# Node maxima of a graph attention layer: destination terms split and keyed during the gathers, maxima in two halves, copies shared with ScalarE

## The chip, the cores and the metric

One NeuronCore of a Trainium2 chip runs the whole program in one launch. The metric is the device time of that core in microseconds (us). TensorE is called PE, VectorE DVE, ScalarE ACT, GpSimd POOL and SyncE SP. The engines run their own instruction streams and meet at semaphores; each stage of the kernel is a block that ends with a barrier over all engines.

## The reference, cut to what matters

Two graph layers on 6250 nodes (128 features) and 106,250 edges sorted by destination. The change touches the first layer's attention, for 4 relations and 8 heads:

```python
es = einsum('nhd,hd->nh', x, a_s); ed = einsum('nhd,hd->nh', x, a_d)      # x = node_inp @ W[r]
logit = leaky_relu(es[src] + ed[dst], 0.2)
logit = where(mask[:, None], logit, -1e30)        # mask: edges of relation r
mx = maximum(segment_max(logit, dst, num_segments=N), -1e30)
p = exp(logit - mx[dst]) * mask[:, None]
alpha = p / segment_sum(p, dst)[dst]
out = segment_sum(alpha[..., None] * x[src], dst)
```

Leaky ReLU grows with its argument and `ed[dst]` is the same for all edges of a destination, so `mx` is `leaky(max(es[src]) + ed)`: the maximum over edges needs only the source terms. The kernel uses this.

## The kernel before, in words

`lists` builds the schedule, `node_inputs` makes the source and destination terms of every node, and `relation_maxima` runs a segmented maximum of the source terms along the sorted edges and stores the running maxima in HBM (`T.run`, 32 floats an edge: 4 relations x 8 heads). Then comes `node_maxima`, the stage that is changed, and after its barrier `relation_attention`, the stage that uses its results; `node_update` and the second layer follow.

`node_maxima` holds nodes as 50 tiles of 128 (a tile is a column of 128 partitions).

- POOL issues 50 indirect DMAs (L857), one a tile: each partition fetches the running maximum at its node's last edge, 32 floats, into `run`. All increment one semaphore.
- DVE first makes `none` (L863: 0 for a node that has edges, -1e30 otherwise), copies the destination terms `K.ed` into slot 0 of `both` (L866) and clears the accumulator `acc` of the next stage (L867, 27,200 floats a partition). Then it waits for all 50 gathers.
- In 5 chunks of 10 tiles it adds `none` (L872), tests which relations are present (L874), adds `ed` (L876) and applies the leaky ReLU into slot 1 of `both` (L877). Each instruction of a chain waits for the one before it (`L.link`).
- `both`, 3200 floats a partition, is then written as a sum of TERMS = 3 bf16 numbers. For each term i: cast to `term` (L885), subtract it from `both` (L887, not for the last), and 16 copies (L890) that bring `term` from node order (partition = node within the tile) to key order in `K.edm` (partition = relation x 32 + node within a window of 32). The copy for (q, r) takes partitions 32q to 32q+31 of `term` and writes partitions 32r to 32r+31 of `K.edm`: 50 tiles x 16 bf16. The next term's cast waits for all 16.
- SP loads two small index tables (L850, L851). ACT and PE have nothing to do in this stage.

`relation_attention` starts with a load of key rows by ACT (L1020) and of edge rows by SP (L930); `K.outside`, a float array of `relation_maxima`, is dead by then and its space holds the edge rows.

Every term of the DVE chain is on the way to the barrier once the gathers have landed. The order of instructions on each engine is the order in which the source writes them.

Of the kernel before, what the change touches and what calls it, by code (L numbers as in the profile page):

```python
# [4 lines left out]
F32, I32, BF16 = mybir.dt.float32, mybir.dt.int32, mybir.dt.bfloat16  # L5
ALU = mybir.AluOpType
ACT = mybir.ActivationFunctionType
# [3 lines left out]
P = 128  # L11
N_NODES, N_EDGES = 6250, 106250
C = 128
R, H, D = 4, 8, 16
# [5 lines left out]
TILES = 50  # L20
# [4 lines left out]
KWIN = 32  # L25
# [11 lines left out]
TERMS = 3  # L37
# [8 lines left out]
BIG = 1e30  # L46
SLOPE0, SLOPE1 = 0.2, 0.01
# [3 lines left out]
def flat(ap):  # L51
    return ap.rearrange("p a b -> p (a b)")
# [776 lines left out]
def node_maxima(nc, K, T, acc):  # L829

    with Phase(nc, "top") as ph:
        CH = 10
        S2 = 2 * H
        run = ph.sb("run", [P, TILES, R * H])
        none = ph.sb("none", [P, TILES])
        both = ph.sb("both", [P, TILES, R, 2, H])
        term = ph.sb("term", [P, TILES, R, 2, H], BF16)
        s_run, s_keyed = (ph.sem(n) for n in ("run", "keyed"))
        s_w, w_all = ph.loads(K, 2)
        block = ph.block()  # L840
        KQ = P // KWIN
        quads = [(q, r) for q in range(KQ) for r in range(R)]

        def to_keys(q, r, i):
            out = K.edm[r * KWIN:(r + 1) * KWIN, :, i * S2:(i + 1) * S2].rearrange("k (t q) c -> k t q c", q=KQ)[:, :, q, :]
            return out, term[q * KWIN:(q + 1) * KWIN, :, r, :, :].rearrange("p t s h -> p t (s h)")

        @block.sync
        def _(sp):
            sp.dma_start(K.reg_kw[:, :], T.ksched_w.rearrange("(a s) -> a s", a=1)).then_inc(s_w, 16)  # L850
            sp.dma_start(K.reg_ke[:, :], T.ksched_e.rearrange("(a s) -> a s", a=1)).then_inc(s_w, 16)  # L851
            sp.wait_ge(s_w, w_all)

        @block.gpsimd
        def _(pool):
            for t in range(TILES):
                pool.indirect_dma_start(run[:, t, :], None, T.run,  # L857
                                        bass.IndirectOffsetOnAxis(ap=K.last[:, t:t + 1], axis=0)).then_inc(s_run, 16)

        @block.vector  # L860
        def _(dve):
            L = K.setup.on(dve)
            L.link(dve.tensor_scalar(none[:, :], K.has[:, :], 1.0, BIG, ALU.subtract, ALU.mult))  # L863
            ed4 = K.ed[:, :, :].rearrange("p t (r h) -> p t r h", r=R)
            run4 = run[:, :, :].rearrange("p t (r h) -> p t r h", r=R)
            L.mark(dve.tensor_copy(both[:, :, :, 0, :], ed4))  # L866
            L.mark(dve.memset(acc[:, :, :], 0.0))  # L867
            dve.wait_ge(s_run, 16 * TILES)
            for c in range(0, TILES, CH):
                k = slice(c, c + CH)  # L870
                wr = "p t r h -> p (t r) h"
                L.link(dve.tensor_tensor(run4[:, k, :, :], run4[:, k, :, :],  # L872
                                         none[:, k].unsqueeze(2).unsqueeze(3).to_broadcast([P, CH, R, H]), ALU.add))
                L.mark(dve.tensor_scalar(K.valid[:, k, :], run4[:, k, :, 0], -0.9 * BIG, None, ALU.is_gt))  # L874
                L.wait()
                L.link(dve.tensor_tensor(run4[:, k, :, :], run4[:, k, :, :], ed4[:, k, :, :], ALU.add))  # L876
                L.mark(dve.scalar_tensor_tensor(both[:, k, :, 1, :], run4[:, k, :, :], SLOPE0, run4[:, k, :, :], ALU.mult, ALU.max))  # L877
            L.wait()
            all4 = "p t r s h -> p (t r s h)"
            rest = both[:, :, :, :, :].rearrange(all4)  # L880
            for i in range(TERMS):
                part = term[:, :, :, :, :].rearrange(all4)
                if i:
                    dve.wait_ge(s_keyed, i * len(quads))
                L.link(dve.tensor_copy(part, rest))  # L885
                if i < TERMS - 1:
                    L.mark(dve.tensor_tensor(rest, rest, part, ALU.subtract))  # L887
                for q, r in quads:
                    out, src = to_keys(q, r, i)
                    dve.tensor_copy(out, src).then_inc(s_keyed, 1)  # L890
                L.wait()
            dve.wait_ge(s_keyed, TERMS * len(quads))


def relation_attention(nc, K, T, acc):

    with Phase(nc, "att") as ph:
        U, RG = U4, 4
        GROUPS = KSTEPS // U
        S2 = 2 * H  # L900
        xe = flat(K.outside[:, :, :])[:, 0:RG * U * XW].rearrange("p (b u c) -> p b u c", b=RG, u=U)
        keyrow = ph.sb("keyrow", [P, RG, U * P], BF16)
        away = ph.sb("away", [P, U * P])
        keyT = ph.sb("keyT", [P, RG, U * P], BF16)
        dv = ph.sb("dv", [P, U, S2])
        keys = ph.sb("keys", [P, RG, U])
# [5 lines left out]
        px = ph.sb("px", [P, 2, U, XR])  # L912
        dst_ps = [ph.ps(f"dst_ps{b}", [P, U, TERMS * S2]) for b in range(2)]
        sum_ps = [[ph.ps(f"sum_ps{b}{q}", [P, 2, XR]) for q in range(U // 2)] for b in range(2)]
# [33 lines left out]
        def _(dve):  # L948
# [3 lines left out]
            def select(j, b, step):  # L952
# [13 lines left out]
                else:  # L966
                    dve.wait_ge(s_sc, j * 3 + 3)
                    if past(j, RG):
                        dve.wait_ge(s_p, j - RG + 1)
                    dve.tensor_tensor(arg[:, b, :, :], leaky[:, :, :], dv[:, :, H:S2], ALU.subtract).then_inc(s_arg, 1)  # L970

# [88 lines left out]
def node_update(nc, K, T, acc):  # L1060

    with Phase(nc, "upd") as ph:
        CH = 4
        bias = ph.sb("bias", [P, C])
        RT = 4
        zero = ph.sb("zero", [P, 4 * HID])
        rden = ph.sb("rden", [P, RT, CH, H])
        tmp = ph.sb("tmp", [P, RT, CH, C])
        s_b, s_c, s_n, s_g, s_gd, s_z, s_zd = (ph.sem(n) for n in ("b", "c", "n", "g", "gd", "z", "zd"))
# [766 lines left out]
def build(nc, T):  # L1836
# [6 lines left out]
    with Phase(nc, "k") as ph:  # L1843
# [13 lines left out]
        with Phase(nc, "l0") as l0:  # L1857
            K.key = l0.sb("key", [P, P * KKC])
            K.last, K.has = l0.sb("last", [P, TILES], I32), l0.sb("has", [P, TILES])
            K.ed, K.valid = l0.sb("ed", [P, TILES, R * H]), l0.sb("valid", [P, TILES, R])  # L1860
            K.index, K.outside = l0.sb("index", [P, NB], I32), l0.sb("outside", [P, NB, R])
            lists(nc, K, T)
            node_inputs(nc, K, T)
            relation_maxima(nc, K, T)
            acc = l0.sb("acc", [P, KSLOTS, XR])
            with Phase(nc, "l0a") as l0a:
                K.reg_kw, K.reg_ke = l0a.sb("reg_kw", [1, P * KKC], I32), l0a.sb("reg_ke", [1, P * KKC], I32)
                K.edm = l0a.sb("edm", [P, KSLOTS, TERMS * 2 * H], BF16)
                node_maxima(nc, K, T, acc)
                relation_attention(nc, K, T, acc)  # L1870
            node_update(nc, K, T, acc)
# [59 lines left out]
```

## Time and profile before

| | |
|---|---|
| median of 3 runs | 5624.1 us (5619.86 to 5625.64) |
| profiled execution, time | 5625.34 us |
| its span | 5623.5 us |
| busy share of the span | DVE 69%, POOL 69%, PE 59%, PEld 41%, ACT 25% |
| the stage `node_maxima` in the trace | about 1441 to 1547 us |

How to read it: the rows below are from one profiled execution. In the timeline view the columns are start (us), duration (us), engine, line, operation, output<-input, count; in brackets stands how long the engine sat idle before it and what released it. In the view of one tile the three durations are minimum, median and maximum in ns. "issue" is time in which the engine waited for nothing that the profile shows.

### The profile page before, as it was taken

The page shows a single profiled execution, that of the slowest core. Times are in us where ns is not written, and L with a number is a line of the kernel's source. Part 1 is how long each engine was busy: PE and PEld are TensorE (multiplying, and loading weights), DVE is VectorE, ACT ScalarE, POOL GpSimd, SP SyncE. Part 2 cuts the span into 40 slices and gives each one's busy share as a digit, 9 for nine tenths or more (in the row PEclk, how much of TensorE's full clock was granted, in tenths as well). Part 3 has the DMA queues.
Part 4 walks back from the last instruction along what each step waited for, and adds up shares of the span by engine and source line. Part 5 has one row for each costly group of instructions (what it writes and reads, how often), then busy time and mean ns, then how long its engine had stood idle before and what let it go on. Part 6 is the DMA issues. An engine that isn't in the chain of part 4 may idle for free. (4 is left out here: it accounts for less than half of the span.)

```text
span 5623.5 us, 106320 instructions
## 1 busy us (share of the span) xinstructions
PE 3324.9 (59%) x16923; PEld 2283.8 (41%) x16924; DVE 3907.1 (69%) x11806; ACT 1426.7 (25%) x2966; POOL 3884.4 (69%) x3803
## 2 busy tenths in 40 slices
PE   0062222222066677155777777777777777777768
PEld 0031111111056566143444444444444455544447
DVE  4635555555578888896777777777777777777765
ACT  0130000000066666334222222222222222222222
POOL 3127777777499999520677777777777777777760
PEclk9885555555577777577888888888889998888889
DMA  2266666666166666323787777877888878778864
GB/s 57 58 186 192 196 195 194 195 193 195 46 154 154 155 153 154 114 49 117 183 176 174 175 172 173 176 173 173 175 175 176 176 174 174 173 172 174 174 141 143
DMA packets 725286, 893.97 MB, mean 159 GB/s; under 512 B 123241, under 2 KB 555465, under 8 KB 724710
## 3 DMA queue, kind: packets, MB, share of 16 engines
q0 software_dynamic: 217200, 396.10, 34.5%
q1 hardware_dynamic: 450742, 392.89, 24.4%
q10 hardware_dynamic: 56976, 101.87, 5.9%
q14 instruction: 357, 2.92, 0.2%
q8 instruction: 11, 0.18, 0.0%
HBM read 652.36 MB, written 238.06 MB: 158 GB/s over the span
## 5 line engine op out<-in xcount | busy, mean ns | idle before, releaser
L1529 POOL DMA_INDIRECT sums<-msg_bsum,k_sidx x831 | 1320.8, 1589 | 378.0 <-issue 242.1
L731 POOL DMA_INDIRECT max_xe<-rows,l_index x832 | 798.5, 960 | 427.0 <-issue 253.3
L1664 PEld LDWEIGHTS msg_both_ps<-msg_onehot,msg_hid 128*128 128x128 f32 x3712 | 555.6, 207 | 1312.5 <-DVE msg_bsum L1573 852.5
L1629 ACT ACTIVATE msg_low_ps<-msg_xs 128x512 f32<-128x512 f32 x928 | 558.1, 601 | 2084.5 <-DVE msg_xs L1598 2049.5
L1543 POOL DMA_INDIRECT msg_ga<-ab,k_bsrc x832 | 827.4, 994 | 369.2 <-issue 201.9
L1677 PE MATMUL msg_pre_ps<-msg_rw,msg_lt 128*128 128x512 f32 x1856 | 1019.0, 632 | 9.5 <-DMA msg_rw<-ab 9.5
L1664 PE MATMUL msg_both_ps<-msg_onehot,msg_hid 128*128 128x64 f32 x3712 | 619.0, 293 | 618.8 <-DVE msg_bsum L1573 602.5
L942 POOL TENSOR_SCALAR att_keyhot<-k_ramp,att_keys 128x128 f32<-128x128 f32 x1028 | 701.6, 701 | 55.6 <-ACT att_keys L1014 54.8
L1608 DVE TENSOR_TENSOR msg_hid<-msg_xs,msg_low_ps 128x512 f32<-128x512 f32 x928 | 636.7, 686 | 97.6 <-ACT msg_low_ps L1629 70.5
L1666 PE MATMUL msg_both_ps<-msg_hid,msg_same 128*128 128x256 f32 x1856 | 653.6, 436 | 0.0
L1597 DVE TENSOR_TENSOR msg_xs<-msg_pre_ps,msg_ga 128x256 f32<-128x256 f32 x928 | 390.1, 420 | 370.0 <-issue 252.9
L1054 PE MATMUL att_sum_ps<-att_px,att_keyhot 128*128 128x136 f32 x2056 | 434.7, 370 | 143.8 <-DVE att_px L976 136.7
L1573 DVE SCALAR_TENSOR_TENSOR msg_bsum<-msg_bsum,l_cont,msg_both_ps 128x256 f32 x928 | 441.2, 475 | 4.8 <-issue 0.2
L1054 PEld LDWEIGHTS att_sum_ps<-att_px,att_keyhot 128*128 128x128 f32 x2056 | 366.3, 255 | 177.4 <-DVE l_acc L986 121.5
L814 PE MATMUL max_mT_ps<-k_ident,max_m 128*32 128x128 f32 x832 | 194.0, 413 | 386.6 <-DVE max_m L748 386.6
L1598 DVE TENSOR_TENSOR msg_xs<-msg_pre_ps,msg_ga 128x256 f32<-128x256 f32 x928 | 385.6, 416 | 3.7
L1677 PEld LDWEIGHTS msg_pre_ps<-msg_rw,msg_lt 128*128 128x128 f32 x1856 | 359.8, 204 | 59.1 <-issue 10.5
L986 DVE TENSOR_TENSOR l_acc<-l_acc,att_sum_ps 128x136 f32 x1028 | 299.5, 291 | 121.1 <-issue 78.8
L748 DVE TENSOR_TENSOR max_m<-max_xe,l_outside 128x256 f32<-128x256 f32 x104 | 44.3, 426 | 441.8 <-DMA max_xe<-rows,l_index 441.8
L823 PE MATMUL max_runT_ps<-k_ident,max_run 32*128 32x32 f32 x832 | 106.9, 288 | 379.7 <-DVE max_run L761 379.7
L1666 PEld LDWEIGHTS msg_both_ps<-msg_hid,msg_same 128*128 128x128 f32 x1856 | 306.9, 208 | 0.0
L802 ACT ACTIVATE max_runT<-max_runT_ps 128x256 f32<-128x256 f32 x104 | 39.8, 383 | 1025.8 <-PE max_runT_ps L823 1025.8
(292 smaller groups left out, 5373.3 us busy)
## 6 DMA issues: line engine op xcount, KB each, us to landing
msg_rw<-ab SPq DMA_DIRECT2D x928, 128.0 KB
l_outside<-xe SPq DMA_DIRECT2D x1028, 72.0 KB, 2.7
xe<-max_xe SPq DMA_DIRECT2D x104, 576.0 KB, 3.0
max_src<-srcs ACTq DMA_DIRECT2D x104, 512.0 KB, 3.9
att_keyrow<-key ACTq DMA_DIRECT2D x257, 128.0 KB, 3.5
msg_lt<-in_efT SPq DMA_DIRECT2D x928, 32.0 KB
rows<-node_rows SPq DMA_DIRECT2D x50, 288.0 KB, 2.4
max_begin<-begin ACTq DMA_DIRECT2D x104, 128.0 KB
```

The source lines that it names most:

```text
L731: pool.indirect_dma_start(xe[:, b, u, :], None, T.rows, bass.IndirectOffsetOnAxis(ap=K.index[:, k:k + 1], axis=0)).then_inc(s_xe[b], 16)
L942: pool.tensor_scalar(keyhot[:, b, u, :], K.ramp[:, 1:P + 1], keys[:, b, u:u + 1], None, ALU.is_equal).then_inc(s_kh, 1)
L1054: pe.matmul(sum_ps[b % 2][u // 2][:, u % 2, :], keyhot[:, b, u, :], px[:, b % 2, u, :], start=True, stop=True).then_inc(s_sum, 1)
L1529: pool.indirect_dma_start(T.sums[k % 2], bass.IndirectOffsetOnAxis(ap=K.sidx[:, k:k + 1], axis=0), bsum[:, (k + 1) % SB, :], None, compute ...
L1543: pool.indirect_dma_start(ga[:, (k + 1) % RB, :], None, T.ab, bass.IndirectOffsetOnAxis(ap=K.bsrc[:, k:k + 1], axis=0)).then_inc(s_ga[k % ...
L1573: dve.scalar_tensor_tensor(row, row, K.cont[:, ds(n, 1)], bwd_ps[u % 2][:, :], ALU.mult, ALU.add).then_inc(s_bs, 1)
L1597: dve.tensor_tensor(xs[:, u % 2, 0:HID], pre_ps[u % 2][:, 0:HID], row[:, HID:2 * HID], ALU.add)
L1608: dve.tensor_tensor(hid[:, b % 2, u, :], xs[:, u % 2, :], low_ps[u % 2][:, :], ALU.max).then_inc(s_hid, 1)
L1629: act.activation(low_ps[u % 2][:, :], xs[:, u % 2, :], ACT.Copy, scale=SLOPE1).then_inc(s_low, 1)
L1664: pe.matmul(fwd_ps[u % 2][:, q * WIN:(q + 1) * WIN], hid[:, b % 2, u, HID + q * P:HID + (q + 1) * P], onehot[:, b, u, :], start=True, stop ...
L1666: pe.matmul(bwd_ps[u % 2][:, :], same[:, b % 2, u, :], hid[:, b % 2, u, 0:HID], start=True, stop=True).then_inc(s_edge, 1)
L1677: pe.matmul(pre_ps[u % 2][:, :], lt[:, b, u, :], rw[:, b % 2, u, :], start=True, stop=True).then_inc(s_pre, 1)
```

## The change

The destination terms and the maxima are no longer joined in `both`. There are three parts: part 0 is the destination terms of all 50 tiles, parts 1 and 2 are the maxima of tiles 0 to 24 and 25 to 49. Each part is split into its three bf16 terms in one go (`split`), with `term` large enough that nothing is overwritten, and then copied to key order; slot s of a term now has its own copy (8 bf16 a tile where it was 16), so that there are 3 parts x 3 terms x 16 = 144 copies where there were 48. DVE does q = 0, 1 and ACT q = 2, 3, 24 copies a part each. Part 0 is done before the memset and before the wait for gathers; its float remainder lies in the space of `K.outside`. The gathers of the two halves have a semaphore each. The chain of none, presence, ed and leaky is done on 25 tiles at a time, in place in `run`.

```diff
+        rest = flat(K.outside[:, :, :])[:, 0:TILES * RH].rearrange("p (t c) -> p t c", t=TILES)
-        both = ph.sb("both", [P, TILES, R, 2, H])
-        term = ph.sb("term", [P, TILES, R, 2, H], BF16)
+        term = ph.sb("term", [P, 2, TERMS, TILES, RH], BF16)
...
+        parts = [(0, slice(0, TILES)), (1, slice(0, HALF)), (1, slice(HALF, TILES))]
+        def to_keys(s, i, k, q, r):
+            c = (2 * i + s) * H
+            out = K.edm[r * KWIN:(r + 1) * KWIN, :, c:c + H].rearrange("k (t q) c -> k t q c", q=KQ)[:, k, q, :]
+            return out, term[q * KWIN:(q + 1) * KWIN, s, i, k, r * H:(r + 1) * H]
...
-                                        bass.IndirectOffsetOnAxis(ap=K.last[:, t:t + 1], axis=0)).then_inc(s_run, 16)
+                                        bass.IndirectOffsetOnAxis(ap=K.last[:, t:t + 1], axis=0)).then_inc(s_run[t // HALF], 16)
+        @block.scalar
+        def _(act):
+            for g, (s, k) in enumerate(parts):
+                act.wait_ge(s_term, g + 1)
+                for i in range(TERMS):
+                    for q in range(KQ // 2, KQ):
+                        for r in range(R):
+                            out, src = to_keys(s, i, k, q, r)
+                            act.activation(out, src, ACT.Copy).then_inc(s_keyed, 1)
...
+            def split(g, values):
+                s, k = parts[g]
+                for i in range(TERMS):
+                    part = term[:, s, i, k, :]
+                    ins = dve.tensor_copy(part, values[:, k, :])
+                    if i < TERMS - 1:
+                        L.link(ins)
+                        L.link(dve.tensor_tensor(values[:, k, :], values[:, k, :], part, ALU.subtract))
+                    else:
+                        ins.then_inc(s_term, 1)
+                dve.wait_ge(s_term, g + 1)
+                for i in range(TERMS):
+                    for q in range(KQ // 2):
+                        for r in range(R):
+                            out, src = to_keys(s, i, k, q, r)
+                            dve.tensor_copy(out, src).then_inc(s_keyed, 1)
+
+            L.mark(dve.tensor_scalar(none[:, :], K.has[:, :], 1.0, BIG, ALU.subtract, ALU.mult))
+            L.link(dve.tensor_copy(rest[:, :, :], K.ed[:, :, :]))
+            split(0, rest)
             L.mark(dve.memset(acc[:, :, :], 0.0))
-            dve.wait_ge(s_run, 16 * TILES)
-            for c in range(0, TILES, CH):
...
+            for g in range(1, len(parts)):
+                s, k = parts[g]
+                n = k.stop - k.start
+                dve.wait_ge(s_run[g - 1], 16 * n)
+                L.link(dve.tensor_tensor(run[:, k, :], run[:, k, :], none[:, k].unsqueeze(2).to_broadcast([P, n, RH]), ALU.add))
+                L.mark(dve.tensor_scalar(K.valid[:, k, :], run[:, k, 0:RH:H], -0.9 * BIG, None, ALU.is_gt))
                 L.wait()
...
+                L.link(dve.tensor_tensor(run[:, k, :], run[:, k, :], K.ed[:, k, :], ALU.add))
+                L.link(dve.scalar_tensor_tensor(run[:, k, :], run[:, k, :], SLOPE0, run[:, k, :], ALU.mult, ALU.max))
+                split(g, run)
             L.wait()
...
+            dve.wait_ge(s_keyed, KEYED)
```

## Rows read from the trace of the kernel before

**Rows 1.** The page: busy us of each engine, share of the span, instructions.

```profile
PE 3324.9 (59%) x16923; PEld 2283.8 (41%) x16924; DVE 3907.1 (69%) x11806; ACT 1426.7 (25%) x2966; POOL 3884.4 (69%) x3803
```

**Rows 2.** Busy us by stretch: from:to, length, each engine, PE clock, DMA share, GB/s.

```profile
1438.00:1507.00 69.00, 0.54 (x6) 0.40 (x4) 26.10 (x19) 0.38 (x1) 47.65 (x50) 0.50 0.08 14
1507.00:1515.50 8.50, 0.00 (x0) 0.00 (x0) 7.97 (x20) 0.00 (x0) 0.00 (x0) 0.50 0.00 0
1515.50:1547.00 31.50, 0.00 (x0) 0.00 (x0) 29.55 (x53) 0.00 (x0) 0.00 (x0) 0.50 0.00 0
```

**Rows 3.** Timeline, the start of the stage.

```profile
1441.20 0.19 DVE L863 TENSOR_SCALAR top_none<-l_has 128x50 f32<-128x50 f32 x1 [0.94 <-PEq L181]
1441.43 0.99 DVE L866 COPY top_both<-l_ed 128x1600 f32<-128x1600 f32 x1
1441.82 1.42 POOL L857 DMA_INDIRECT top_run<-run,l_last  x1 [12.81 <-PEq L181]
1448.04 22.73 DVE L867 MEMSET l_acc<- 128x27200 f32 x1 [5.61 <-issue]
```

**Rows 4.** Timeline, from the last gather's landing to the next stage.

```profile
1506.97 0.49 DVE L872 TENSOR_TENSOR top_run<-top_run,top_none 128x320 f32<-128x320 f32 x1 [36.21 <-DMA top_run<-run,l_last]
1507.49 0.20 DVE L874 TENSOR_SCALAR l_valid<-top_run 128x40 f32<-128x40 f32 x1
...
1515.52 1.83 DVE L885 CAST top_term<-top_both 128x3200 bf16<-128x3200 f32 x1
1517.38 3.49 DVE L887 TENSOR_TENSOR top_both<-top_both,top_term 128x3200 f32<-128x3200 f32 x1
1520.79 6.23 DVE L890 COPY l0a_edm<-top_term 32x800 bf16<-32x800 bf16 x16
...
1540.57 6.23 DVE L890 COPY l0a_edm<-top_term 32x800 bf16<-32x800 bf16 x16
1547.37 1.30 ACTq L1020 DMA_DIRECT2D att_keyrow<-key  x3
```

**Rows 5.** The view of tile run: the gathers and their time to landing.

```profile
L857 POOL DMA_INDIRECT top_run<-run,l_last x50: 940/944/1424, 1441.8 to 1503.5; - x50
...
DMA to landing us min/median/max: 2.2/2.4/3.5
```

**Rows 6.** The view of tile term: the copies to key order.

```profile
L890 DVE COPY l0a_edm<-top_term x48: 349/360/367, 1520.8 to 1546.4; 32x800 bf16<-32x800 bf16 x48
```

**Rows 7.** Timeline, early in the program: other gathers beside long DVE instructions.

```profile
24.06 3.79 DVE L467 TENSOR_TENSOR list_begin<-list_rec 104x1024 f32<-104x1024 int32 x1
26.18 2.74 POOL L399 DMA_INDIRECT list_dst<-in_dst,list_block_i  x1 [0.18 <-issue]
27.88 0.69 DVE L468 TENSOR_SCALAR list_begin<-list_begin 104x1024 f32<-104x1024 f32 x1
28.49 1.96 DVE L469 SCALAR_TENSOR_TENSOR list_index<-list_rec 104x1024 f32<-104x1024 int32 x1
29.21 2.09 POOL L399 DMA_INDIRECT list_dst<-in_dst,list_block_i  x1 [0.30 <-issue]
```

**Rows 8.** Timeline, in relation_maxima: a gather beside short DVE instructions.

```profile
704.42 0.35 DVE L769 SCALAR_TENSOR_TENSOR max_junk<-max_src,max_srcf,k_upto 128x128 bf16<-128x128 f32 x1
704.53 1.06 POOL L731 DMA_INDIRECT max_xe<-rows,l_index  x1 [0.30 <-issue]
```

**Rows 9.** Groups by line and shape on ACT: busy us, mean ns, idle before.

```profile
L1117 ACT ACTIVATE l_acc<-upd_tmp 128x512 f32 x44 | 27.7, 630 | 55.5 <-POOL upd_tmp L1108 55.5
L627 ACT ACTIVATE node_squares<-node_x 128x3200 f32<-128x3200 f32 x2 | 5.7, 2870 | 30.8 <-DVE node_x L595 30.8
L438 ACT ACTIVATE k_loc<-list_tp_ps 128x512 f32<-128x512 f32 x2 | 2.0, 1131 | 0.0
```

**Rows 10.** Timeline of ACT, two instructions in a row with no wait.

```profile
1992.38 0.72 ACT L1030 ACTIVATE att_keyT<-att_away,k_ones 128x512 bf16<-128x512 f32 x1
1993.01 0.19 ACT L1014 ACTIVATE att_keys<-l_key 128x4 f32 x1
```

More of the change, by code:

```diff
@@ L831, in node_maxima @@
     with Phase(nc, "top") as ph:
-        CH = 10
-        S2 = 2 * H
-        run = ph.sb("run", [P, TILES, R * H])
+        HALF = TILES // 2
+        KQ = P // KWIN
+        RH = R * H
+        run = ph.sb("run", [P, TILES, RH])
+        rest = flat(K.outside[:, :, :])[:, 0:TILES * RH].rearrange("p (t c) -> p t c", t=TILES)
         none = ph.sb("none", [P, TILES])
-        both = ph.sb("both", [P, TILES, R, 2, H])
-        term = ph.sb("term", [P, TILES, R, 2, H], BF16)
-        s_run, s_keyed = (ph.sem(n) for n in ("run", "keyed"))
+        term = ph.sb("term", [P, 2, TERMS, TILES, RH], BF16)
+        s_run = [ph.sem(f"run{q}") for q in range(2)]
+        s_term, s_keyed = (ph.sem(n) for n in ("term", "keyed"))
         s_w, w_all = ph.loads(K, 2)
         block = ph.block()
[L841 to L846, printed above, removed]
+        parts = [(0, slice(0, TILES)), (1, slice(0, HALF)), (1, slice(HALF, TILES))]
+        KEYED = len(parts) * TERMS * KQ * R
+        def to_keys(s, i, k, q, r):
+            c = (2 * i + s) * H
+            out = K.edm[r * KWIN:(r + 1) * KWIN, :, c:c + H].rearrange("k (t q) c -> k t q c", q=KQ)[:, k, q, :]
+            return out, term[q * KWIN:(q + 1) * KWIN, s, i, k, r * H:(r + 1) * H]
         @block.sync
@@ L862, in _ @@
             L = K.setup.on(dve)
[L863 to L866, printed above, removed]
-            L.mark(dve.memset(acc[:, :, :], 0.0))
-            dve.wait_ge(s_run, 16 * TILES)
-            for c in range(0, TILES, CH):
[L870 to L874, printed above, removed]
+            def split(g, values):
[14 more added lines that the diff above has]
+                            dve.tensor_copy(out, src).then_inc(s_keyed, 1)
@@ L875, in _ @@
                 L.wait()
-                L.link(dve.tensor_tensor(run4[:, k, :, :], run4[:, k, :, :], ed4[:, k, :, :], ALU.add))
-                L.mark(dve.scalar_tensor_tensor(both[:, k, :, 1, :], run4[:, k, :, :], SLOPE0, run4[:, k, :, :], ALU.mult, ALU.max))
+                L.link(dve.tensor_tensor(run[:, k, :], run[:, k, :], K.ed[:, k, :], ALU.add))
+                L.link(dve.scalar_tensor_tensor(run[:, k, :], run[:, k, :], SLOPE0, run[:, k, :], ALU.mult, ALU.max))
+                split(g, run)
@@ L878, in _ @@
             L.wait()
[L879 to L891, printed above, removed]
@@ L892, in _ @@
-            dve.wait_ge(s_keyed, TERMS * len(quads))
+            dve.wait_ge(s_keyed, KEYED)
 def relation_attention(nc, K, T, acc):
```

## The prediction

> **What bounds the kernel now.** I read the page first: no engine is busy for more than 69% of the span [rows 1], so the kernel is a row of stages with different limits, and only the changed stage's own limit counts. The busy time by stretch shows it: from 1438 to 1507 us POOL is busy 47.65 of 69 us with 50 gathers, and from 1507 to 1547 DVE alone works (7.97 of 8.5, 29.55 of 31.5) and every other engine and the DMA stand at 0 [rows 2]. The timeline puts edges on it: the gathers start at 1441.82, the last is issued at 1503.5 and landed at 1506.97, when DVE had been idle for 36.21 us [rows 3 to 5]; the last copy ends about 1546.8 and the next stage begins at 1547.37 [rows 4]. So the stage is gathers (65.5 us), then a serial DVE tail (39.8 us); both are on the path, and the cover of one engine by another in it is nil.
>
> One row needs care. The memset is shown as 22.73 us after 5.61 us in which DVE waited for nothing [rows 3]. Their sum, 28.34 us, is 27,200 elements at 0.96 a ns, so I take it that the memset runs from 1442.42 to 1470.77 and its start is recorded late. I use 28.3 us.
>
> **Durations.** From the copy of 1600 floats, 0.99, and the cast of 3200, 1.83 [rows 3, 4], a one-input DVE instruction on floats costs 0.162 + 0.52 us per 1000; from 320 at 0.49 and 3200 at 3.49 a two-input one costs 0.157 + 1.042 per 1000 [rows 4]. The key copy of 800 bf16 takes 0.360 [rows 6]; with the same fixed part it is 0.25 per 1000, so 400 take 0.26 and 200 take 0.21. Sixteen of them span 6.23 us, a pitch of 0.391, thus 0.031 beyond the duration. Chained instructions start 0.03 after the end before them (1506.97 + 0.49 to 1507.49) [rows 4].
>
> **The tail that stays behind the last gather (part 2).** Chain on 800 floats: five two-input instructions (none, ed, leaky, two subtractions) at 0.99, three casts at 0.58, presence 0.23; with 0.03 after each of the nine, 4.95 + 1.74 + 0.23 + 0.27 = 7.2 us. Then DVE has 24 copies of 200 elements at 0.24, 5.7 us, and ACT 24 beside it. The trace has no ACT copy of this shape. From 512 floats at 630 ns and 3200 at 2870 ACT costs 0.203 + 0.833 per 1000 [rows 9], 0.37 for 200. ACT instructions without a wait start 0.09 before the end of the one in front (0.63 after 1992.38 where the duration is 0.72) [rows 10]; where partitions change, DVE loses such an overlap [rows 6], and ACT may too. The pitch is therefore 0.28 to 0.40, and I take 0.34, the middle, since neither row is nearer: 8.2 us. If ACT pays for short pieces as it does for a scattered output (512 elements in 1131 ns, 1.81 per 1000 [rows 9]), it is 0.56, 13.5 us. The pieces here are 8 neighbours long, nearer to the plain rows, so this end is for the range. ACT ends last: tail 7.2 + 8.2 = 15.4 us where it was 39.8. That removes **24.4 us** (bounds: DVE's own 12.9, 26.9 saved; scattered ACT, 19.1 saved).
>
> **What moves ahead of that.** Part 0 on DVE: the copy of 1.0 us was there already; new are three casts at 0.99 and two subtractions at 1.83, with gaps 6.8 us, and 24 copies at 0.29, 7.0 us. The memset moves behind it, to about 1456.3 to 1484.6. Part 1 is 7.2 + 5.7 = 12.9 us, to 1497.5; its 25 gathers would land by 1476, so the memset, not the gathers, decides when it starts. All of this must fit before the last landing, 1506.97, and does with 9.5 us to spare. ACT's copies (24 of 400 elements, at 0.45 to 0.57, and 24 of 200) fit in the same cover, and ACT is idle here. If that cover were gone, every us beyond 9.5 would be one on the path. SP's two loads are untouched; queued behind DVE's new instructions are only the memset and its own chain. The barrier is now released by ACT's last copy through DVE's wait, about 0.1 us. The second half's semaphore changes nothing for the last landing.
>
> **What it costs POOL.** The price of the cover is that DVE now works beside the gathers, where before only one copy and the memset did. The rows show what that does. The first gather, beside the copy, took 1.42 against a median of 0.944: it ended 0.82 after that copy [rows 3, 5]. An earlier one took 2.74 beside a two-input and then a one-input instruction and ended 0.35 after the second; the next took 2.09 and ended 0.85 after a two-input one [rows 7]. Beside 0.35-us instructions a gather loses 0.1 (1.06) [rows 8]. Beside the memset (no input) the gathers keep 0.94 [rows 5]. A reading that fits: 0.09 us in, a gather needs a read that any DVE instruction with two inputs or with a fast copy holds up until its end; 0.5 us later it needs writes, some 0.35 us, which only the fast one-input kind holds up.
>
> Stepping the gathers with this through part 0's chain: they start at 1441.82, 1444.1, 1447.0 and 1449.9, where the fourth started at 1446.04 before: +3.8 us. Through part 1's chain the same steps give 5 gathers in 8.3 us instead of 6.25: +2.0. Beside the back-to-back copies (7.0 + 5.7 us, with 0.03 between them) the trace has nothing; from below 0.1 a gather [rows 8], some 1 us in all; from above no progress at all, 12.7 us. I take 0.35 for each of some 8 gathers (half a copy's wait for the read, one for the writes), 2.8 us, near the lower end because rows 8 is the only case of short instructions. Sum **+8.6 us**; bounds 1.0 and 18.5.
>
> The Trainium skill has a stricter rule (SBUF — State Buffer, Who interferes with whom): a Vector copy or cast in a two-port mode takes the pair of ports shared with GpSimd for the whole instruction, and the other "fully blocks", the descriptors of a gather included. The 1.42 and 2.74 above agree with that. The page does not say how a run of short ones shares; taken as lock-out for all DVE work in the two parts it is the third rival.
>
> **Sum.** Profiled execution 5625.34 (span 5623.5) - 24.4 + 8.6 = 5609.5. The median of the runs shown lies 1.2 below it: 5608.3. I forecast **5609 us**, 16 us faster (0.28%). Nothing behind the barrier changes but its start.
>
> **Rivals.**
> 1. The gathers are not noticeably held up (+1): 5601. For: gathers at 0.94 beside the memset and at 1.06 beside short ones. Against: the 1.42, 2.74 and 2.09. Chance 0.17.
> 2. The copies starve the gathers nearly wholly (+14 to 18), or ACT pays for short pieces on top: gain 3 to 10, 5614 to 5621, say 5618. For: 0.03 us gaps leave POOL little. Against: rows 8. Chance 0.27.
> 3. The other side: every DVE instruction of parts 0 and 1 locks POOL out for its whole length, 6.8 + 7.0 + 7.2 + 5.7 = 26.7 us. It decides once the last landing slips by more than 24.4 us: 5625.3 + 2.3 = 5627.6, and with ACT at 0.56 5633. Against: a gather beside a two-input instruction finished within 0.85 of its end, so it isn't set back, and its last part runs beside such instructions. Chance 0.05.
> 4. The change doesn't do what it says: ACT's copies wait for something, or part 1 starts late (the memset ends after the gathers), so that parts 1 and 2 run one after another: 12.9 us more in the tail, 5622. The 9.5 us of slack speaks against it. Chance 0.03.
>
> The forecast itself has 0.48.
>
> **Chances.** A difference below 0.2%, 11.2 us, is what a measurement of this kernel can tell from none. Faster by more: the forecast nearly whole and rival 1, 0.63. Within 0.2%: rival 2, 3, 4 and the forecast's upper edge, 0.34. Slower by more than 0.2%: 0.03, since even the lock-out with a dear ACT stays below 5635. The range that holds the time 8 times in 10 is 5600 to 5621.
>
> **What would show it.** The last gather landing near 1515.6 instead of 1506.97, with gathers of 1.2 to 2.5 us beside part 0 and part 1 and 0.94 beside the memset; DVE copies of 0.26 and 0.21 us; ACT copies of 0.37 at a pitch of 0.28 to 0.40; from the last landing to the first load of the next stage 15.5 us. Wrong would be: gathers that need over 3 us beside copies (rival 2), a landing at 1508 (rival 1), an idle ACT between copies, or a DVE that is still busy with part 1 when the last gather lands.

## The result, and where the time went

The changed kernel takes 5586.8 us (median of 5; 5579.8 to 5603.2) against 5625.5 for the kernel before (5 runs, 5619.9 to 5630.9): ratio 0.9937, 95% interval 0.9919 to 0.9955. That is 38.7 us faster where 16 were forecast, and below the predicted range. The profiled run took 5584.6 (span 5582.8, where it was 5623.5).

I cut both traces at the first instruction that an engine runs in each stage; 2.3 us behind the last row's end belong to no stage in either kernel. The sum of the differences is the difference of the spans, -40.7 us:

| us | start of the stage | node maxima | attention | update | mixing | edge input | messages | output |
|---|---|---|---|---|---|---|---|---|
| before | 1441.2 | 109.4 | 720.4 | 100.4 | 220.1 | 95.4 | 2799.3 | 135.0 |
| after | 1440.4 | 90.7 | 718.3 | 100.3 | 222.4 | 94.3 | 2779.2 | 134.9 |

So the changed stage gives 18.7 us, near the 15.8 of the prediction, and 20.1 come from the message stage, in which no line was changed. The rest of this text has two parts for these two numbers.

**The changed stage.** Busy time by stretch after (columns as in [rows 2]):

```profile
1438.00:1510.90 72.90, 0.00 (x0) 0.00 (x0) 50.58 (x75) 21.66 (x49) 52.41 (x50) 0.50 0.08 13
1510.90:1518.10 7.20, 0.00 (x0) 0.00 (x0) 6.92 (x9) 0.00 (x0) 0.00 (x0) 0.50 0.00 0
1518.10:1528.00 9.90, 0.00 (x0) 0.00 (x0) 4.88 (x24) 8.78 (x24) 0.00 (x0) 0.50 0.00 0
```

Where DVE had 26.10 busy us beside the gathers [rows 2], it has 50.58, and what follows the last landing is 17 us and not 40. The timeline of DVE (answers to [rows 3, 4]):

```profile
1442.51 1.82 DVE L884 TENSOR_TENSOR l_outside<-l_outside,top_term 128x1600 f32<-128x1600 f32 x1
1444.37 0.99 DVE L881 CAST top_term<-l_outside 128x1600 bf16<-128x1600 f32 x1
...
1461.30 22.73 DVE L897 MEMSET l_acc<- 128x27200 f32 x1 [5.73 <-issue]
...
1487.41 0.58 DVE L881 CAST top_term<-top_run 128x800 bf16<-128x800 f32 x1
1488.02 0.99 DVE L884 TENSOR_TENSOR top_run<-top_run,top_term 128x800 f32<-128x800 f32 x1
...
1491.30 6.04 DVE L892 COPY l0a_edm<-top_term 32x200 bf16<-32x200 bf16 x24
1510.88 0.99 DVE L902 TENSOR_TENSOR top_run<-top_run,top_none 128x800 f32<-128x800 f32 x1 [13.54 <-DMA top_run<-run,l_last]
...
1518.13 5.60 DVE L892 COPY l0a_edm<-top_term 32x200 bf16<-32x200 bf16 x24
```

and that of ACT beside and behind it:

```profile
1518.13 9.34 ACT L871 ACTIVATE l0a_edm<-top_term 32x200 bf16<-32x200 bf16 x24 [17.50 <-DVE top_term L881]
1528.04 1.31 ACTq L1037 DMA_DIRECT2D att_keyrow<-key  x3
```

Part 1 is done 13.54 us before the last gather lands; part 2's chain takes 7.25 us, DVE's copies 5.60, ACT's 9.34, and ACT ends last. The gathers, on POOL, are slower beside some of DVE's work only:

```profile
1440.97 1.62 POOL L860 DMA_INDIRECT top_run<-run,l_last  x1 [12.82 <-PEq L181]
1442.90 2.58 POOL L860 DMA_INDIRECT top_run<-run,l_last  x1 [0.30 <-issue]
1445.78 2.58 POOL L860 DMA_INDIRECT top_run<-run,l_last  x1 [0.30 <-issue]
1448.67 0.96 POOL L860 DMA_INDIRECT top_run<-run,l_last  x1 [0.30 <-issue]
...
1487.48 1.32 POOL L860 DMA_INDIRECT top_run<-run,l_last  x1 [0.30 <-issue]
...
1490.75 1.33 POOL L860 DMA_INDIRECT top_run<-run,l_last  x1 [0.30 <-issue]
1492.38 0.94 POOL L860 DMA_INDIRECT top_run<-run,l_last  x1 [0.30 <-issue]
```

They are held up beside the first copy and part 0's chain (1440.5 to 1448.2) and beside the casts of part 1's (1487.4 to 1491.3), not beside the copies to key order that follow each. The two of 2.58 began under a two-input instruction of 1.82 and ended 0.1 after the cast behind it; the three of 1.32 to 1.34 each began under a cast of 0.58. The two before these, begun near the end of a two-input instruction of 0.99, took 0.96 and 1.01. Landing comes 4.8 us later in the stage.

**The message stage.** DVE's loop there handles 16 steps of messages an iteration, in 47.6 us, 55 times over. In the kernel before, the turn of an iteration looks like this on DVE:

```profile
4010.38 0.68 DVE L1608 TENSOR_TENSOR msg_hid<-msg_xs,msg_low_ps 128x512 f32<-128x512 f32 x1
4015.29 0.17 DVE L1556 COPY msg_hl<-l_src_hl 128x8 bf16 x1 [4.22 <-issue]
4015.41 0.42 DVE L1557 TENSOR_TENSOR msg_onehot<-k_ramp,k_loc 128x256 f32<-128x256 f32 x1
4020.53 0.42 DVE L1597 TENSOR_TENSOR msg_xs<-msg_pre_ps,msg_ga 128x256 f32<-128x256 f32 x1 [4.69 <-issue]
```

The first instruction behind the loop's backward branch comes 4.22 us late, and "issue" says that it waited for nothing that the profile shows. (The second gap, 4.69, stands behind a load of the schedule's registers and is in every kernel here.) The view of tile msg_hl sums the first gap. Before and after:

```profile
L1556 DVE COPY msg_hl<-l_src_hl x232: 160/164/512, 2686.8 to 5435.6; 128x8 bf16 x112, 128x8 bf16<-128x8 bf16 x4
  issue: 225.9, 55
```
```profile
L1573 DVE COPY msg_hl<-l_src_hl x232: 158/161/466, 2666.3 to 5394.7; 128x8 bf16 x112, 128x8 bf16<-128x8 bf16 x4
  issue: 201.7, 55
```

4.1 us each before, 3.7 after. I call it the head stall. POOL, which scatters the sums, waited 102.0 us for DVE's msg_bsum at the scatters in the kernel before, and 75.7 after. So the change took 24 us of stall from a loop that it doesn't touch. The experiments ask why.

### The profile page after: what moved, and what is told of

Read it like the earlier page. It is cut to its first block and busy times, and to the rows that moved or that the text cites. A ratio compares the mean times of both kernels' runs of the same rounds, so it can differ in the third digit from the quotient of the medians.

```text
span 5582.8 us, 106412 instructions
## 1 busy us (share of the span) xinstructions
PE 3325.9 (60%) x16923; PEld 2280.0 (41%) x16924; DVE 3904.2 (70%) x11828; ACT 1453.4 (26%) x3038; POOL 3888.0 (70%) x3803
```

## The experiments

In every set the kernel before ran on the same chip, and the ratio is to it. Three sets were disturbed: in the one of r5 to r8 it took 6120 us itself, in those of r9 to r12 and of r17 and r18 6021 and 6011. In the traces of those sets the changed stage starts 250 to 285 us later than here; what disturbed them, no run shows. Their times and message-stage lengths are not set against others; the stalls and the changed stage can be. "Messages" below is the time from the first scatter to the last (2748.7 before, 2728.3 after).

**r1: the changed kernel once more.** No edit.

> The changed kernel again. In its first profile the changed stage gives 18.5 us and the edge message stage, which nobody touched, another 20.5. Theory C (chance: the message stage takes a different time in every execution, and the first profile was a lucky one): the stage again about 87.7 us long, the message stage (first to last scatter, 2748.7 us before, 2728.3 after) anywhere between 2725 and 2750. Theory P (position: the stage's new instructions shift where later code lies, and the message loop runs better from there): 2728 again within 5, and the median again 35 to 42 us below the kernel before.

5594.9 us, ratio 0.9936 [0.9922, 0.9949]. Stage 90.9, head stall 207.0 in 55, messages 2741.3. The stage repeats to 0.2 us; the message stage is 7.4 us shorter than in the kernel before, where it was 20.4 in the first profile.

**r2: the kernel before, only padded** to the changed kernel's number of instructions on DVE and ACT (in the node-maxima stage, under the gathers):

```
+            for n in range(72):
+                act.activation(pad2[:, 4 * n:4 * n + 4], K.part[:, 0:1].to_broadcast([P, 4]), ACT.Copy)
...
+            for n in range(22):
+                dve.memset(pad[:, 4 * n:4 * n + 4], 0.0)
```

> The kernel before with 72 tiny ScalarE copies and 22 tiny VectorE memsets added in node_maxima, into scratch that nobody reads, under the cover of the gathers: as many instructions on each engine as the changed kernel has, no other change. The stage stays 106 us. Theory P: the message stage falls to 2728 and the whole kernel is about 20 us (0.36%) faster than before. Theory C: ratio 1.000 within 0.002, message stage near 2749 like before or scattered.

5618.0, 0.9979 [0.9970, 0.9988]; stage 109.4, head stall 208.5 in 55, messages 2741.9. Nothing of the change is in it, yet the stall falls to 3.8 us, as in r1, and the time by 9.5, half of what I expected. Little of the stall that went reached POOL: up to 5480 us its waits for msg_bsum at the scatters are 106.0, against 107.8 before, 78.5 after and 90.5 in r1.

**r3: the changed kernel with its stage made long again**: most of the accumulator's memset moved behind part 2.

```
-            L.mark(dve.memset(acc[:, :, :], 0.0))
+            L.mark(dve.memset(acc[:, 0:70, :], 0.0))
...
+            L.link(dve.memset(acc[:, 70:KSLOTS, :], 0.0))
```

> The changed kernel, with 130 of the 200 slots of the accumulator cleared after the last copy instead of during the gathers: 17,680 elements, 18.4 us more in the tail, so the stage lasts as long as before (106 us), with the changed kernel's instructions (one memset more). If all that the stage saves is its own time: 18.4 us slower than the changed kernel. Theory P: 5605, 20 us below before. Theory T (time: the later stages gain because they begin earlier): back to 5625. Theory C: between 5600 and 5625.

5612.4, 0.9973 [0.9961, 0.9984]; stage 110.1, head stall 206.4, messages 2734.8. The message stage starts as late as before (2722.4 us, 2724.3 before) and keeps the lower stall and a gain of 13.9 us: the hour at which it starts is not the cause.

**r4: the changed kernel without ScalarE's share**, all 72 + 72 copies on DVE.

```
-                    for q in range(KQ // 2):
+                    for q in range(KQ):
```

> The changed kernel without ScalarE's share: DVE makes all 48 copies of each part. By the profile of the changed kernel DVE's pitch is 0.23 us at 25 tiles against 0.39 for ScalarE, so the tail behind the last gather is 7.2 + 48 x 0.233 = 18.4 us instead of 16.6: 2 us slower than the changed kernel. By my prediction (ScalarE at 0.34, DVE at 0.24) it would be 7.2 + 11.5 against 15.4, 3.3 slower. Theory P adds another code position and so up to 20 us either way; theory C adds nothing to the median beyond its scatter of some 10 us.

5516.8, 0.9806 [0.9793, 0.9820]. The stage is 93.0, 2.3 more than with ScalarE, and the kernel 78 us faster than the changed one, where I had allowed for 20 at most. The view of tile msg_hl again:

```profile
L1563 DVE COPY msg_hl<-l_src_hl x232: 158/161/508, 2666.8 to 5313.6; 128x8 bf16 x112, 128x8 bf16<-128x8 bf16 x4
its engine sat idle before it (us, times) until:
  PEq L181: 5.9, 1
```

The head stall is gone in all 55 iterations (what is left is the stage's start), and messages take 2657.3. r4 has 69 more instructions on DVE than r2 and 72 fewer on ACT, which led to the next set.

**r5 to r8: how many, and on which engine.** The kernel before with 94 and with 58 memsets on DVE and with 72 activations on ACT, as in r2; the changed kernel with 72 memsets on DVE.

> The kernel before with 94 tiny VectorE memsets into scratch, under the cover of the gathers: the number of VectorE instructions that the version without ScalarE's share has ahead of the later stages; nothing else changes. In the message loop VectorE stalls 3.4 to 5.3 us at the first instruction after each of 55 backward branches (226 us before, 201 to 208 in the changed kernel, 0 without ScalarE's share). Theory P: the place of that code, set by the number of VectorE instructions ahead of it, makes the stall; it goes to 0 here, the message stage to about 2657 us and the whole to about 5535 (ratio 0.984). Theory A: ScalarE's copies, or the code behind them, cost the message stage time, and leaving them out gave it back: no effect here, ratio 1.000.

> The kernel before with 58 tiny VectorE memsets, the middle between 22 (stall 3.7 us at each branch) and 94 (no stall). Theory P without more: either near 3.7 us a branch (ratio about 0.997) or near none (0.984), as the border lies above or below; a value in between would say that the cost falls gradually with the place. Theory A: 1.000.

> The kernel before with 72 tiny ScalarE copies and nothing on VectorE. Theory P (VectorE's place): VectorE's stalls stay 226 us, ratio 1.000 within 0.001. If ScalarE's code place made the 9 us of the padded kernel: 0.998.

> The changed kernel, ScalarE's share and all, with 72 tiny VectorE memsets behind the accumulator's (some 4 us under the cover of the gathers, of which VectorE has 13.5 us left). VectorE's later code lies where it does without ScalarE's share. Theory P: the branch stalls go to 0 and the whole to about 5515, 2 us faster than the version without ScalarE's share. Theory A: stays at 5591.

Head stalls: r5, r6 and r8 none, r7 227.0 us in 55 (225.9 in the kernel before). Times 5878.2, 5878.8, 6120.7 and 5878.4; ratios 0.9601 [0.9574, 0.9628], 0.9587 [0.9554, 0.9621], 1.0007 [0.9982, 1.0031], 0.9602 [0.9578, 0.9625]. So 72 instructions more on ACT change nothing, and 58 on DVE take the stall away. Why the stall's end is worth 240 us in this set, and 90 in the undisturbed one of r13, no run shows. As a side result the small memsets did not stay cheap: the first 22 are quick as in r2 (0.35 us), the others came one every 0.7 or 1.4 us while gathers ran. The view of the pads' tile in r5:

```profile
L870 DVE MEMSET top_pad<- x94: 62/62/62, 1734.1 to 1775.4; 128x4 f32 x94
its engine sat idle before it (us, times) until:
  issue: 38.3, 35
```

**r9 and r10** repeat r8 and r5 beside the next two.

> The changed kernel with 72 tiny VectorE memsets again, since in the set before this one the kernel before itself took 6120 us, with waits on transfers in many stages. With the kernel before at 5625 again: theory P (place of VectorE's code) 5515, message stage near 2657, no stall behind the branches; if the large gain belonged to the disturbed set: 5590.

> The kernel before with 94 tiny VectorE memsets again, for the same reason. Theory P: message stage near 2657, total 5535. Together with the version without ScalarE's share (5517) this gives the change's own part free of the place: stage 93 against 109, 16 us.

5804.4 and 5806.0, 0.9646 [0.9624, 0.9667] and 0.9651 [0.9628, 0.9674], without head stalls. The stages were 107.8 and 113.5 us, long by the slow pads: in r9 part 1 began only after all gathers. So they can't show what the change is worth with the place made equal.

**r11: a shorter tail.** Halves of 38 and 12 tiles, and one copy for each block and relation that carries the three terms at once, 10 on DVE and 6 on ACT, with 114 memsets in the stage.

```
-        HALF = TILES // 2
+        HALF = 38
...
+            out = K.edm[r * KWIN:(r + 1) * KWIN, :, :].rearrange("k (t q) (i s h) -> k t q i s h", q=KQ, s=2, h=H)[:, k, q, :, s, :]
+            return out, term[q * KWIN:(q + 1) * KWIN, s, :, k, r * H:(r + 1) * H].rearrange("p i t h -> p t i h")
```

> A version made from the profiles: the maxima in 38 and 12 tiles, so that less is left behind the last gather; one copy for all three terms of a (q, r), so 16 copies a part instead of 48; VectorE makes 10 and ScalarE 6; and 114 tiny VectorE memsets that put the later code where no branch stalls. Tail behind the last landing: chain on 384 floats 4.4 us and ten copies of 288 elements at 0.26, or six of ScalarE at 0.46, 2.8 us: 7.2 against 16.6 us, so the stage about 81 us. Total 9 us below the changed kernel with 72 memsets (about 5506). If the copies lose their fast mode with the third dimension: 10 x 0.49, 2 us more. If part 1 isn't done when the last gather lands, up to 4 us more.

5806.4, 0.9649 [0.9626, 0.9672]. Part 2 is 7.2 us from its start to its last copy, as hoped, but the pads delayed part 1 and the stage took 101.1. Its form comes back in r15.

**r12: which work of DVE holds a gather up.** The kernel before, with 16 short copies, 3 long casts on 32 partitions and 16 short copies on 32 partitions put between memsets under the gathers (a single execution).

> Only the port question. The kernel before, in whose wait for the gathers VectorE now runs, behind the memset: 16 short float copies on 128 partitions (200 elements, 0.26 us each, back to back), 3.1 us of memset, 3 long casts on 32 partitions (1600 elements, 1.0 us each), memset, 16 short float copies on 32 partitions. Gathers take 0.94 alone, 1.3 to 2.6 beside long casts and two-input instructions on 128 partitions, and 0.94 beside the short bf16 copies on 32 partitions. Theory S (short ones leave room, whatever the partitions): 0.94 to 1.05 beside both kinds of short copies, 1.3 to 1.6 beside the long ones. Theory N (few partitions don't hold the gather up): 0.94 beside everything on 32 partitions, over 1.1 beside the short ones on 128. Theory L (lock-out): no gather ends while short copies run on 128 partitions.

6016.2 us. DVE's and POOL's timelines of the same stretch:

```profile
1744.48 3.28 DVE L871 COPY l_outside<-l_ed 128x200 f32<-128x200 f32 x16
1750.92 3.01 DVE L875 CAST top_term<-l_ed 32x1600 bf16<-32x1600 f32 x3
1757.21 3.32 DVE L878 COPY l_outside<-l_ed 32x200 f32<-32x200 f32 x16
```
```profile
1744.76 0.98 POOL L857 DMA_INDIRECT top_run<-run,l_last  x1 [0.30 <-issue]
1746.04 0.95 POOL L857 DMA_INDIRECT top_run<-run,l_last  x1 [0.30 <-issue]
...
1751.05 2.00 POOL L857 DMA_INDIRECT top_run<-run,l_last  x1 [0.30 <-issue]
1753.35 1.41 POOL L857 DMA_INDIRECT top_run<-run,l_last  x1 [0.30 <-issue]
...
1757.56 0.95 POOL L857 DMA_INDIRECT top_run<-run,l_last  x1 [0.30 <-issue]
```

Back-to-back copies, one every 0.2 us, cost a gather at most 0.04, on 128 partitions as on 32; casts of 1 us cost 1.06 and 0.47. So the share of time that DVE is busy doesn't decide. I put it down to the length of the single instruction; the short ones are copies and the long ones casts, but the long copy in the kernel before held a gather up too (1.42, [rows 3]). The memsets, of 22.73 and of 2.55 us, hold none up. The message loop moved here as well: its head stall is 192.8 us in 55, the shortest of all.

**r13 and r16: the place alone.** The memsets now stand in the edge-input stage, where DVE idles for 9.6 us. Nothing of the node maxima is touched, and of the loops ahead of the messages only one of 13 instructions, in the edge-input stage itself, moves.

```
+            for n in range(94):
+                dve.memset(pad[:, 4 * n:4 * n + 4], 0.0)
             dve.wait_ge(s_loc0, 1)
```

> The kernel before, with 94 memsets of 16 bytes a partition on VectorE in the edge-input stage, ahead of its wait for edgein_loc_ps: VectorE stands idle there for 9.6 us, and they take about 6 to 8. The stage of the node maxima is untouched and no earlier loop moves; only the message loop's place among VectorE's instructions moves, by 94. Theory of place: node-maxima stage 109.4 us as before, stall of 4.1 us at the head of each message iteration gone, message stage (scatters first to last) 2657 to 2665 us in place of 2741 to 2749, time 65 to 90 us shorter, about 5550. Rival (what counts is what VectorE does just ahead of or in the node-maxima stage, or that the loops before it moved): stall and time stay, 5625.

> The kernel before with 40 such memsets at the same place: between the +22 at which the head stall was still 3.7 us and the +58 at which it was gone. Theory of place: either 3.3 to 3.7 us a head (it falls with the place: message stage 2725 to 2740, time 5605 to 5620) or none (a border lies between +22 and +40: 2657 to 2665, 5550). I lean to none, 0.55. Rival: 5625.

r13: 5535.7, ratio 0.9836 [0.9823, 0.9850]. Stage 109.5, messages 2660.5, and the turn of an iteration:

```profile
4007.56 0.68 DVE L1611 TENSOR_TENSOR msg_hid<-msg_xs,msg_low_ps 128x512 f32<-128x512 f32 x1
4008.16 0.16 DVE L1559 COPY msg_hl<-l_src_hl 128x8 bf16 x1
4008.23 0.42 DVE L1560 TENSOR_TENSOR msg_onehot<-k_ramp,k_loc 128x256 f32<-128x256 f32 x1
```

90 us from 94 instructions that compute nothing and take 2.2 us in all. The stall that went is 226 us, the message stage 88 shorter: the rest was hidden behind other work. TensorE's granted clock rose too (from 2750 to 5350 us 0.89 in the kernel before, 0.94 in r13); what part of the 88 is the clock's is not separated. POOL's waits for msg_bsum at the scatters, before and in r13:

```profile
POOL sums L1529 <- DVE msg_bsum L1573: 102.0, 80, 9.5
```
```profile
POOL sums L1532 <- DVE msg_bsum L1576: 40.8, 76, 9.1
```

r16 (40 memsets) went the other way: 5634.9, 1.0014 [1.0005, 1.0023]; head stall 219.9 in 55, the gap behind it 5.25 in the mean where it was 4.86, messages 2768.6. I had leaned to "no stall" with 0.55. "Later is better" had thus failed; the next table gives the loop's place in the compiled stream of DVE, counted in the program that the compiler writes and not in a trace (every instruction, waits and branches too; the loop is 316 long).

| loop begins at | kernels | head stall |
|---|---|---|
| 2419, 2420 | before, r7 | 4.1 us |
| 2440 to 2442 | after and r1, r3, r2 | 3.7 to 3.8 |
| 2457 | r12 | 3.5 |
| 2458 | r16 | 4.0 |
| 2477 | r6 | none |
| 2511 to 2513 | r4, r5, r8 to r11, r13, r14, r15 | none |

**r14: the change with the place made equal**, 72 such memsets in the edge-input stage of the changed kernel. **r15: the best version**, r11's form with 114 of them there.

> The changed kernel with 72 such memsets at the same place in the edge-input stage, so that the message loop stands 94 instructions later than in the kernel before. Theory of place: stage 91 us, no head stalls, message stage 2657 to 2665, time 5510 to 5522, that is 65 to 80 under the changed kernel. Rival: as the changed kernel, 5587 to 5595.

> The changed kernel with the maxima in parts of 38 and 12 tiles, one copy for each 32-partition block and relation that takes all three terms (10 on VectorE, 6 on ScalarE), and 114 memsets in the edge-input stage. What stands behind the last gather should be 7 us and not 17: stage 80 to 83 us. Theory of place: message stage 2657 to 2665 as above, time 5500 to 5512. If place counted for nothing: 5577 to 5590.

r14: 5513.9, 0.9804 [0.9790, 0.9817]; stage 90.8, messages 2660.0, no head stall. Against r13, in the same set and without a stall in either, the change is worth 21.9 us, 18.7 of them in its stage. r15: 5512.5, 0.9794 [0.9780, 0.9807]; its tail on DVE:

```profile
1515.21 0.56 DVE L900 TENSOR_TENSOR top_run<-top_run,top_none 128x384 f32<-128x384 f32 x1 [6.02 <-DMA top_run<-run,l_last]
...
1519.59 2.54 DVE L890 COPY l0a_edm<-top_term 32x288 bf16<-32x288 bf16 x10
```

The stage is 84.4, 6.4 under r14's, but attention took 722.4 (718.6 in r14) and the edge input 97.0 (93.1), and the two times can't be told apart. Why those stages were longer is open. r15 is 2.1% faster than the kernel before, and all but some 23 us of that is the place.

**r17 and r18: a rule for the place.** Suppose that the stream is cut in blocks of 256 instructions, as the Trainium skill has it (Runtime: NRT & Kernel Launch, Instruction fetch mechanics). A loop of 316 instructions then lies over two blocks or over three; it does the latter for 59 starts of each 256. The table allows one such band, with its end between 2458 and 2476. Two kernels outside the table test it: r15's form with no memset at all (start 2398, ahead of the band) and the kernel before with 257 memsets (start 2675, 256 behind its own).

> The version of r15 with no memsets added anywhere. Counted in the compiled stream of VectorE (every instruction, waits and branches too) the message loop is 316 instructions long and begins at number 2419 in the kernel before, 2440 to 2442 in the changed one, r2 and r3, and 2458 in r16, all with the head stall; at 2477 in r6 and 2511 to 2513 in r4, r5, r8 and r13 to r15, all without it. Here it begins at 2398, ahead of all these. Theory of blocks (the Trainium skill, Runtime: NRT and Kernel Launch, Instruction fetch mechanics: an engine holds two blocks of 256 instructions, and a taken branch to a target outside them waits for a transfer): the loop stalls where its 316 instructions lie over three blocks, which is a band of 59 starts; the runs put the upper end of the band at 2458 to 2476, so its lower end at 2400 to 2418, and 2398 is free: no head stall, message stage 2657 to 2665 us, stage 84 us, time 5505 to 5515. Rival (the later the loop stands, the better): stall of 4 us as before, message stage 2725 to 2770, time 5575 to 5615.

> The kernel before with 257 tiny memsets in the edge-input stage: the message loop begins at 2675 in place of 2419, exactly 256 later. They take 6 us by the 2.2 of r13's 94, in the idle time of 9.6. Theory of blocks: the same place in a block as before, so the head stall is back at 4.1 us, message stage 2741 to 2769, time 5615 to 5640. Rival (the later the better, or far enough is enough): no stall, message stage 2657 to 2665, time about 5536 as r13.

r17: 5795.7, 0.9635 [0.9606, 0.9663], stage 84.4, messages 2670.9. r18: 6013.8, 1.0012 [0.9989, 1.0035], messages 2851.0. The times are those of a disturbed set; the stall needs no comparison. In r17 (first fence) there is none, in r18 it is what it was in the kernel before:

```profile
L1571 DVE COPY msg_hl<-l_src_hl x232: 158/159/480, 2939.9 to 5611.6; 128x8 bf16 x112, 128x8 bf16<-128x8 bf16 x4
its engine sat idle before it (us, times) until:
  PEq L181: 5.9, 1
```
```profile
L1559 DVE COPY msg_hl<-l_src_hl x232: 158/160/519, 2961.5 to 5813.4; 128x8 bf16 x112, 128x8 bf16<-128x8 bf16 x4
its engine sat idle before it (us, times) until:
  issue: 225.7, 55
```

Both forecasts of the stall held, the one of its size too (225.7 us in 55, 225.9 in the kernel before), and "later is better" failed twice. The times that I forecast can't be judged in this set.

The profile shows the transfers behind it. Its section on DMA has a queue of the kind "instruction"; the first line is from the page of the kernel before, the second from r13's (packets, MB, share of 16 engines):

```profile
q14 instruction: 357, 2.92, 0.2%
```
```profile
q14 instruction: 83, 0.68, 0.0%
```

The nine pages with the head stall have 357 to 360 of these packets, the eleven without it 82 to 84. In the message stage it is 324 of 8 KB in each of the nine traces and 49 in each of the eleven; the difference, 275, is 5 for each of the 55 iterations. In all nine, such a packet ends inside every one of the 55 head stalls, and DVE starts again 1.7 to 1.8 us (median) after the last has ended. The trace doesn't name the engine that a packet is for, but I know no other reading: in the stall DVE waits for its own instructions, and "issue" is what the profile prints for it.

The Trainium skill (Runtime: NRT & Kernel Launch, Instruction fetch mechanics) states that an engine holds two blocks of 256 instructions, and that a taken branch to a target outside them must wait for a transfer. All eighteen runs agree with it, by head stalls of 3.5 to 4.1 us in the mean inside the band, none outside, and by the 275 packets. What sets the size inside the band is open: at 2419, 2420 and 2675 (4.1 us) mostly two packets end within a stall, at 2440 to 2458 one, but that leaves 3.5 at 2457 beside 4.0 at 2458.

## Why the prediction was wrong

**The step that failed** is "Nothing behind the barrier changes but its start". The change adds 21 entries to DVE's stream ahead of the message loop (start 2419 to 2440). The loop stayed inside the band, but at a place where its head stall is 0.4 us shorter: 225.9 to 201.7 us in 55 iterations. I had put everything behind the barrier at 0; the message stage gave 20.1 of the 40.7 us. r2 has only the added instructions and shows the stall's fall, r3 shows it with a long stage. From first scatter to last the stage became 20.4 us shorter in the first profile, 7.4 in r1, 6.8 in r2 and 13.9 in r3, all against one trace of the kernel before. So the place is shown as a cause, and how much of the 20 is scatter between runs is not settled. The sign was right, and no rival had this mechanism: I weighed instructions only by their duration and cover, never as code. The gap of 4.22 was in the trace of before, 55 times, and I had not looked behind the barrier for it.

**The changed stage**, term by term:
- The memset from its hidden start: 28.34 us predicted, 5.73 + 22.73 = 28.46 measured, and it ended at 1484.03. Right.
- Part 2's chain: 7.2 predicted, 7.25. DVE's copies: a pitch (from one start to the next) of 0.24, measured 0.23. Right.
- ACT's copies: a pitch of 0.34 taken, 0.39 measured, so they don't overlap when partitions change (367 ns each). The upper of my two rows' bounds would have been right. From landing to the next load 17.2 us and not 15.5.
- Gathers: +8.6 taken, +4.8 measured. Part 0's chain cost 3.5 (3.8 taken), part 1's 1.3 (2.0), the copies nothing (2.8). The stepping of a gather through long instructions held; the guess for short ones was wrong, though rows 8 had pointed the right way, and r12 shows it apart. The lower bound of 1.0 left out the 5.8 that I had just stepped for the two chains, so it had no working of its own.
- Sum: -23.2 for the tail and +4.8 for the gathers, -18.5; the stage shows -18.7 where I had -15.8. The two misses partly cancel.
- Rival 1 (gathers not held up) has the total that came nearest, 5601, but by luck: the rest came from the message stage, and in the stage itself the measured -18.7 is nearer to the forecast's -15.8 than to the rival's -23.4. Rivals 2 and 3 fell with the copies, rival 4 with part 1 done 13.54 us before the landing. For rival 3 I had drawn on the Trainium skill (SBUF — State Buffer, Who interferes with whom): "fully blocks" fits the 1-us casts, 2.00 and 1.41, but beside copies of 0.2 us in a row the gathers kept 0.94 to 0.98, and there the measurement decides.
- ScalarE's share: r4 without it has a stage of 93.0 against 90.7, so it is worth 2.3 us, 0.04% of the kernel. On the changed kernel it cost more than it gave: its 72 copies, taken off DVE, left the message loop in the band, and r4 is 78 us faster.

## What to carry to other kernels

Before you price a change, look at the first instruction behind the backward branch of every long loop, the untouched ones too: a gap that comes once an iteration and waits for nothing can be a price of the code's place, and then an edit anywhere ahead on that engine changes it. (The gap behind the register load, 4.7 us, is in every kernel here and is no such price.) When you compare two versions, make the place equal (a few tiny instructions in a stretch where the engine idles, as r13 and r14 have) and then subtract; here the change alone is worth 22 us and the place 90. A count of the packets of the instruction queue on the page tells in a line whether two versions differ in this. Work that reads SBUF, put under gathers, is nearly free for them as many copies of 0.2 us and dear as few instructions of 1 to 2 us.

## What the runs showed of the hardware that I had not expected

- The head of a DVE loop of 316 instructions stalls for 3.5 to 4.1 us an iteration, in the mean, at seven starts from 2419 to 2458 and at 2675, and not at 2398, 2477 or 2511 to 2513. With the stall come 275 more packets of 8 KB on the instruction queue, 5 an iteration.
- 94 memsets of 4 elements a partition take 2.2 us when no gather runs (r13: the first begins at 2602.1, the last at 2604.3), and 41 us beside gathers (r5), 35 of them after idle time that waits for nothing shown. Whether the supply of instructions is slowed by the gathers' transfers was not tried.
- A gather on POOL beside DVE: 2.58 us when begun under a two-input instruction of 1.82 with a cast of 0.99 behind it, 1.32 to 1.34 when begun under a cast of 0.58, 0.94 to 0.98 under copies of 0.2 in a row and under memsets.
- ACT's copies on 32 partitions have a pitch of 0.390 us at 367 ns each where the partitions change, no overlap as in [rows 10].
